# Step one's exponentials in two halves between the copies; the batch's one-hot row blocks behind its selection

## The chip, the cores and the metric

One core of a Trainium2 chip. The metric is the device time of one launch in microseconds (us); the smaller the better. The engines are TensorE (PE), VectorE (DVE), ScalarE (ACT), GpSimd (POOL) and the DMA queues that SyncE (SP) feeds. Each engine runs its own instruction stream in order; streams meet at semaphores only.

## The reference

The input is `x` (3327 nodes by 128) and `adj` (3327 by 3327, sparse in value, stored dense). First comes a graph layer with two steps (`STEPS = 2`), of which this is the core:

```python
for n in range(STEPS):
    q = Xa @ W1.T @ W2.T
    k = Xa @ W3.T
    probs = softmax(q @ k.T, axis=-1)
    # keep, in each row, the largest probabilities until their sum reaches 0.9 (ties by index)
    A = probs * mask
    A = A / A.sum(-1, keepdims=True)
    Xf = R @ Xf                      # R = (adj + I), rows normalised
    Xa = A @ Xa
    Z = Z + Xf @ U1[n].T + Xa @ U2[n].T
```

Then follow layer norms, a signed three-head graph attention over `adj`, two GRU cells and a last layer norm. The change touches only the first graph layer.

## The kernel before

Four programs run one behind the other: `layer0` (the two steps above), `normalize_and_sum`, `attention` and `gates_and_output`. Only `layer0` (L519) matters here. In it the 3327 rows, padded to `NP` = 3328, are 26 tiles of 128 rows, worked in 13 pairs (`PAIRS`), two tiles (`k` = 0, 1) to a pair. A row of logits is 3327 wide and is made in seven chunks of 512 columns (`NC` = 7, the last 256 wide).

What a pair p goes through in step one (`step == 0`):

- PE makes the logits of a tile chunk by chunk into two PSUM banks `lg` (L850). ACT copies each chunk into the tile `e` (L1152, `copy_next_logit`) and so frees its bank. A chunk's matmul waits for the copy of the chunk two before it.
- DVE takes the largest values of each segment of `e` (`tops`, MAX8 at L71), from which the row's maximum and its negative come (`negmax_ready`, L1412), and then sorts out the 48 largest (`sort_tops`, L149 to L157; `tops_ready` behind it).
- ACT turns the row into exponentials in one instruction of 3327 columns with its sum in `total` (`exps`, L1184), and the sorted values too (`exp_tops`, L1196, which waits for `tops_ready`, drains and raises `e_ready`).
- DVE searches the cut (`search`, `solve_sorted`, from L163), PE turns the flags of the search over (`turn_flags`, L902), DVE reads them (L1458) and selects (`select`, `keep` at L450), which raises `w_ready`.
- PE transposes the selected row in seven chunks into the banks `tr` (L966), ACT copies each chunk to `wT` (`copy_weights`, L1230), PE multiplies by the rows of X (L976, tile `small`), and ACT copies the outcome (`copy_row`, L1239).

The order on each engine is written out by hand. While pair p is attended, the logits of pair p + 2 are made, and pair p + 1 has its maxima, exponentials and search. In ACT's `pair`, the exponentials of tile 0 of pair p + 1 stand behind `copy_weights` chunk 4 of tile 0, and ahead of chunks 5 and 6. Those of tile 1 stand behind chunk 2 of tile 1 and ahead of the copy of logit chunk 2; `exp_tops` stands behind chunk 3. Pairs 0 to 10 and pair 12 have logit chunks between the attended ones, pair 11 has none; pair 12 has no exponentials. PE's `pair` puts logit chunks 0 and 1 ahead of attended chunk 5 of tile 0, and chunks 2 to 6 behind the attended chunks 0 to 4 of tile 1. Ahead of pair 0, the prologue makes the projections, the logits of pairs 0 and 1 and the exponentials of pair 0.

Step two (`step == 1`) has another order, in which whole exponentials stay. Rows whose nucleus its quick search can't settle are moved into one extra tile of up to 128 rows, the batch (`taken_batch`, L1526), which runs behind the 13 pairs: DVE takes fine maxima, ACT makes exponentials (L1184) and those of the candidates (L1192), DVE halves 16 times (`solve_halving`) and selects, PE attends, and last PE spreads the 128 results over the 26 tiles (`place_taken`, L953) by one-hot blocks `home`. DVE makes these 26 blocks of 128x128 in `find_homes` (L1521), between its maxima and its search, in the memory of `e[0][1]`.

Of the kernel before, what the change touches and what calls it, by code (L numbers as in the profile page):

```python
# [89 lines left out]
class Search:  # L90

    NAMES = ("total", "whole", "theta", "value", "tau", "lo", "cut", "cut_eff", "cut_kept", "above", "best", "left",
             "over", "up", "known", "reaches", "covers", "partial", "short", "strict", "backward", "cut_dropped", "scale", "levels", "shut", "mass_hi", "rowmax",
             "negmax", "open", "over_full", "spilled", "slot", "blank", "inv_kept0", "inv_kept1", "kept",
             "r_above0", "r_theta", "r_below", "r_was", "r_stays", "r_moves", "r_tau", "r_hi", "r_value", "r_bound",
             "r_above", "r_known", "r_up", "r_mass")

# [421 lines left out]
def layer0(nc, d, dims, H, ident):  # L519
# [7 lines left out]
    PROJ = 3 * NC  # L527
    FIRST_PROJ = NC + 2
    WHOLE = NC - 1
    UNITS = 2 * PAIRS  # L530
    TURN = PAIRS // 2

# [3 lines left out]
    with ExitStack() as ctx:  # L536
# [83 lines left out]
        def seq(step, p, slot):  # L620
            return (p + step * PAIRS) * 2 + slot
# [56 lines left out]
        with nc.Block() as block:  # L678
# [456 lines left out]
            def _(eng):  # L1135
# [4 lines left out]
                for step in range(2):  # L1140
# [40 lines left out]
                    def exps(p, b, k):  # L1181

                        eng.wait_ge(negmax_ready, seq(step, p, k) + 1)
                        eng.activation(e[b][k][:, 0:N], e[b][k][:, 0:N], ACT.Exp, bias=negmax[k],  # L1184
                                       accum_out=total[k])

                    def exp_tops(p):

                        eng.wait_ge(tops_ready, turn_of(step, p) + 1)
                        if at(p, PAIRS):  # L1190
                            tops = find.fine[:, :, :].rearrange("p a b -> p (a b)")
                            eng.activation(tops, tops, ACT.Exp, bias=negmax[0])  # L1192
                        for k in range(0 if at(p, PAIRS) else 2):
                            tops = (find.sorted[:, k, :] if step == 0 else
                                    find.cand[k][:, 0:SEGS[1], :].rearrange("p a b -> p (a b)"))
                            eng.activation(tops, tops, ACT.Exp, bias=negmax[k])  # L1196
                        eng.drain()
                        eng.sem_inc(e_ready, 1)
# [26 lines left out]
                    def copy_weights(p, k, c):  # L1225
                        n = seq(step, p, k) * NC + c
                        sl = cols(c)
                        eng.wait_ge(tr_ready, n + 1)
                        eng.wait_ge(wT_free, n + 1)
                        eng.activation(wT[(k * NC + c) % 2][:, 0:sl.stop - sl.start],  # L1230
                                       tr[(k * NC + c) % 2][:, 0:sl.stop - sl.start],
                                       ACT.Copy).then_inc(wT_ready, 1)
# [22 lines left out]
                    def pair(p, b, rest):  # L1255
                        ahead = rest >= 2 or at(p, PAIRS - 1)
                        for c in range(NC - 2):
                            copy_weights(p, 0, c)
                            if c == 1 and not at(p, 0):
                                copy_kq(p - 1)  # L1260
                        if rest:
                            exps(p + 1, 1 - b, 0)
                        for c in range(NC - 2, NC):
                            copy_weights(p, 0, c)
                        copy_row(p, b, 0)
                        for c in range(NC):
                            copy_weights(p, 1, c)
                            if rest and c == 2:
                                exps(p + 1, 1 - b, 1)
                            if rest and c == 3:  # L1270
                                exp_tops(p + 1)
                            if c == NC - 1:
                                copy_row(p, b, 1)
                            if ahead:
                                copy_next_logit(p, b, 0, c)
                        if ahead:
                            for c in range(NC):
                                copy_next_logit(p, b, 1, c)
                        copy_turned_attended(p)
                        copy_update(p)  # L1280
                        copy_h(p)
# [67 lines left out]
                    if step == 0:  # L1349
                        for c in range(NC):  # L1350
                            project(c, kT[0:DA, :], c)
                        project(NC, h1, 0)
                        project(NC + 1, qT[0:DA, :], 0)
                        for k in range(2):
                            copy_logits(0, 0, k)
                        for c in range(1, NC):
                            project(chunk(0, 0, 1, NC - 1) + c, h1, c)
                        for k in range(2):
                            exps(0, 0, k)
                        for c in range(1, NC):  # L1360
                            project(chunk(0, 0, 1, NC - 1) + NC - 1 + c, qT[0:DA, :], c)
                        exp_tops(0)
                        for k in range(2):
                            copy_logits(1, 1, k)
                    else:
                        for k in range(2):
                            copy_logit(0, 1, k, NC - 1)
                        copy_grid()
                        for k in range(2):
                            exps(0, 1, k)  # L1370
                        exp_tops(0)
                        for k in range(2):
                            copy_logits(1, 0, k)
# [13 lines left out]
            def _(eng):  # L1387
# [12 lines left out]
                for step in range(2):  # L1400
# [19 lines left out]
                    def search(p):  # L1420
                        eng.wait_ge(e_ready, turn_of(step, p) + 1)
                        eng.memset(gate[:, :], 0.0)
                        if step == 0:
                            find.solve_sorted(eng)
                        else:
                            find.solve_halving(eng, [find.cand[k][:, 0:SEGS[1], :].rearrange("p a b -> p (a b)")
                                                     for k in range(2)], HALVINGS)
                            find.end(eng, True, spills=True)
                        eng.sem_inc(flags_ready, 1)
# [33 lines left out]
                    def select(p, b, k):  # L1463
                        find.select(eng, k, e[b][k][:, :], kinds[k], flag, regs, step == 1,
                                    found=step == 1 and not at(p, PAIRS))
                        if step == 1:
                            eng.tensor_tensor(kept[k], kept[k], find.one("blank" if at(p, PAIRS) else "spilled", k),
                                              ALU.add)
                            eng.drain()
                        eng.reciprocal(inv_kept[b][k], kept[k]).then_inc(w_ready, 1)  # L1470
# [34 lines left out]
                        eng.wait_ge(grid_copied, 1)  # L1505
                        eng.tensor_scalar(XR[1][:, :, P], XR[1][:, :, P], row_no, None, ALU.add)

                    def find_homes():

                        eng.wait_ge(taken_copied, 1)  # L1510
                        row_of_slot = find.row_of_slot[:, :]
                        eng.tensor_copy(row_of_slot, taken_rows[:, P:P + 1])
                        eng.drain()
                        eng.tensor_scalar(row_in_tile, XR[1][:, :, P], row_no, row_of_slot, ALU.subtract, ALU.subtract)
                        eng.tensor_scalar(find.one("blank", 0), row_of_slot, 0.5, None, ALU.is_lt)
                        eng.drain()
                        eng.tensor_scalar(row_in_tile, row_in_tile, -1.0, None, ALU.mult)
                        eng.drain()
                        eng.wait_ge(tr_ready, seq(step, PAIRS - 1, 0) * NC)
                        for t in range(T):  # L1520
                            eng.tensor_scalar(home[:, t * P:(t + 1) * P], slot_no, row_in_tile[:, t:t + 1], None,  # L1521
                                              ALU.is_equal)
                        eng.drain()
                        eng.sem_inc(home_ready, 1)

                    def taken_batch():  # L1526
# [7 lines left out]
                        eng.tensor_scalar(negmax[0], rowmax[0], -1.0, None, ALU.mult).then_inc(negmax_ready, 1)  # L1534
                        eng.drain()
                        eng.sem_inc(tops_ready, 1)
                        find_homes()
                        eng.wait_ge(e_ready, turn_of(step, PAIRS) + 1)
                        eng.memset(gate[:, :], 0.0)
                        find.solve_halving(eng, [find.fine[:, :, :].rearrange("p a b -> p (a b)")], FINE_HALVINGS)  # L1540
# [8 lines left out]
                        eng.drain()  # L1549
                        eng.reg_load(kinds[0], find.flag_int[0:1, 0:1])  # L1550
                        select(PAIRS, 0, 0)
                        eng.wait_ge(addedA, 2 * PAIRS)
                        eng.wait_ge(addedR, UNITS)
                        for c in range(NC):
# [913 lines left out]
```

## Time and profile before

| what | us |
|---|---|
| median of 3 runs | 2745.24 (2742.2 to 2754.72) |
| the profiled execution | 2751.88 |
| its span | 2750.1 |
| PE busy in the span | 2367.2 (86%) |
| DVE busy | 2200.9 (80%) |
| ACT busy | 1070.2 (39%) |
| step one's pairs 0 to 11 (69.70 to 505.73) | 436.03 |
| a pair of step one, steady (216.47 to 253.36) | 36.89 |

Times in the rows are us from the span's start. A timeline row has start, length, engine, line, operation, what it writes and reads, the shape, how many such instructions are merged, and in square brackets the idle time of the engine just before and what ended it. "issue" is idle time that no recorded instruction explains. Matmuls are pipelined: in a row of several, the last one's end lies some tenths behind the start of the next group.

### The profile page before, as it was taken

To read this page: it belongs to the slowest core of one execution; us is meant where nothing else is said; L and a number is where in the kernel's file an instruction comes from. 1 tells how busy PE (TensorE), PEld (TensorE's weight loads), DVE (VectorE), ACT (ScalarE), POOL (GpSimd) and SP (SyncE) were. 2 spreads that over 40 slices of the span, in tenths; PEclk is the share of its full clock that TensorE was granted. 3 is DMA by queue.
4 is the path that set the end of the run, shared out by engine and by line. 5 is a ranking of instruction groups with operands and counts; after the bars stand their busy time and mean duration, and the time that the engine had idled before them with its cause. 6 is when DMAs were issued, how large, how long until landed. Compare 5 with 4: busy or idle time off the path is not lost. (4 is left out here: it accounts for less than half of the span.)

```text
span 2750.1 us, 53658 instructions
## 1 busy us (share of the span) xinstructions
PE 2367.2 (86%) x17795; PEld 1996.2 (73%) x17795; DVE 2200.9 (80%) x6636; ACT 1070.2 (39%) x1803; POOL 138.5 (5%) x342
## 2 busy tenths in 40 slices
PE   7999999868889887888887649987999999999985
PEld 2666666556667776767775549985999999999952
DVE  3777777588887888888889677766999999999836
ACT  4666666533323333333332130003434434434323
POOL 0000000101111111000010010000000000000000
PEclk8999999989899998999988869998999999999997
DMA  3000000022122221222221135542333343434220
GB/s 130 2 1 2 1 1 1 2 100 79 73 76 101 92 88 54 97 98 101 101 101 50 52 153 201 201 171 104 127 127 126 116 137 105 146 103 138 91 89 25
DMA packets 57330, 245.05 MB, mean 89 GB/s; under 512 B 6929, under 2 KB 18576, under 8 KB 43344
## 3 DMA queue, kind: packets, MB, share of 16 engines
q1 hardware_dynamic: 57040, 241.99, 25.2%
q8 instruction: 83, 1.36, 0.2%
q14 instruction: 207, 1.70, 0.2%
HBM read 235.15 MB, written 6.82 MB: 88 GB/s over the span
## 5 line engine op out<-in xcount | busy, mean ns | idle before, releaser
L2058 PE MATMUL a_acc<-H,pT 128*128 128x128 f32 x4056 | 548.0, 277 | 10.4 <-ACT a_rows L2090 3.8
L2058 PEld LDWEIGHTS a_acc<-H,pT 128*128 128x128 f32 x4056 | 495.5, 192 | 27.5 <-DVE pT L2192 18.7
L976 PE MATMUL small<-XR,wT 128*128 128x128 f32 x2756 | 373.3, 280 | 29.9 <-ACT wT L1230 29.3
L976 PEld LDWEIGHTS small<-XR,wT 128*128 128x128 f32 x2756 | 339.1, 195 | 45.8 <-ACT wT L1230 45.8
L850 PE MATMUL lg<-kT,qs 128*128 128x512 f32 (+1 forms) x742 | 341.0, 596 | 30.6 <-ACT e L1152 20.4
L71 DVE MAX8 cand<-e 128x8 f32<-128x64 f32 (+3 forms) x1898 | 302.8, 240 | 56.9 <-issue 34.1
L2192 DVE TENSOR_TENSOR pT<-a_tr,a_adjT 128x512 f32<-128x512 f32 (+1 forms) x546 | 316.6, 645 | 22.4 <-PE a_tr L2017 19.2
L880 PE MATMUL accR<-XR,adj 128*128 128x129 f32 x2704 | 327.9, 283 | 0.0
L880 PEld LDWEIGHTS accR<-XR,adj 128*128 128x128 f32 x2704 | 324.7, 200 | 0.0
L2017 PE MATMUL a_tr<-ident,prob 128*128 128x128 f32 x2028 | 312.4, 274 | 10.9 <-ACTq L2084 10.9
L1230 ACT ACTIVATE wT<-tr 128x512 f32<-128x512 f32 (+1 forms) x371 | 206.1, 566 | 246.7 <-PE tr L966 245.7
L2170 DVE CUSTOM_DVE_ANT_0 prob<-a_adj,EB 128x3328 f32<-128x3328 f32 x78 | 282.6, 3623 | 0.0
L850 PEld LDWEIGHTS lg<-kT,qs 128*128 128x128 f32 x742 | 119.0, 194 | 194.2 <-ACT e L1152 148.2
L966 PE MATMUL tr<-ident,e 128*128 128x128 f32 x1378 | 212.2, 281 | 48.7 <-DVE scalars L1470 42.6
L1152 ACT ACTIVATE e<-lg 128x512 f32<-128x512 f32 (+1 forms) x371 | 206.5, 566 | 114.4 <-PE lg L850 112.5
L2017 PEld LDWEIGHTS a_tr<-ident,prob 128*128 128x128 f32 x2028 | 242.1, 142 | 11.1 <-issue 11.1
L2082 ACT ACTIVATE prob<-prob,a_negmax 128x3328 f32<-128x3328 f32 x78 | 238.9, 3063 | 8.9 <-DVE a_negmax L2179 8.9
L966 PEld LDWEIGHTS tr<-ident,e 128*128 128x128 f32 x1378 | 164.8, 145 | 99.7 <-issue 55.1
L1706 PE MATMUL g_sp<-g_adj,H 128*128 128x128 f32 x1352 | 166.2, 286 | 17.2 <-ACTq L1771 17.2
L1706 PEld LDWEIGHTS g_sp<-g_adj,H 128*128 128x128 f32 x1352 | 162.0, 201 | 19.0 <-issue 18.4
L1184 ACT ACTIVATE e<-e,scalars 128x3327 f32<-128x3327 f32 x53 | 162.1, 3060 | 11.3 <-DVE scalars L1534 10.4
L219 DVE SCALAR_TENSOR_TENSOR work<-cand,mid 128x416 f32<-128x416 f32 (+1 forms) x198 | 143.3, 757 | 8.0
(344 smaller groups left out, 2485.1 us busy)
## 6 DMA issues: line engine op xcount, KB each, us to landing
adj<-in_adjT SPq DMA_DIRECT2D x52, 1664.0 KB, 7.2
g_adj<-in_adjT SPq DMA_DIRECT2D x26, 1664.0 KB, 6.8
a_adj<-in_adj SPq DMA_DIRECT2D x26, 1664.0 KB, 6.8
a_adjT<-in_adjT SPq DMA_DIRECT2D x156, 256.0 KB, 3.9
a_adjT<-in_adjT SPq DMA_DIRECT2D x26, 128.0 KB, 4.1
XT<-in_x_t SPq DMA_DIRECT2D x1, 1664.0 KB, 7.1
hT_scratch<-hT SPq DMA_DIRECT2D x1, 1664.0 KB, 12.0
nsT_scratch<-nsT SPq DMA_DIRECT2D x1, 1664.0 KB, 5.3
```

Source lines behind the costliest of these rows:

```text
L71: eng.max(cand[:, n, :], src[:, n * seg:min((n + 1) * seg, width)])
L850: eng.matmul(lg[bank(st, p, k, c)][:, 0:sl.stop - sl.start], qs[k][:, :], kT[:, sl], start=True, stop=True).then_inc(lg_ready, 1)
L880: mm = eng.matmul(accR[:, :], adj[k][:, j * P:(j + 1) * P], xf[:, j, :], start=False, stop=(j == T - 1))
L966: mm = eng.transpose(tr[(k * NC + c) % 2][:, o:o + P], e[b][k][:, j * P:(j + 1) * P], ident[:, :])
L976: mm = eng.matmul(accA[:, :], wT[(k * NC + c - 1) % 2][:, o:o + P], xa[:, j, 0:P], start=(j == 0), stop=(j == T - 1))
L1152: eng.activation(e[b][k][:, sl], lg[bank(st, p, k, c)][:, 0:sl.stop - sl.start], ACT.Copy).then_inc(lg_free, 1)
L1706: mm = eng.matmul(sp[k][:, :], H[:, j, :], adj[q][:, j * P:(j + 1) * P], start=(j == 0), stop=(j == T - 1))
L2017: mm = eng.transpose(tr[g % BANKS][:, (j % 4) * P:(j % 4 + 1) * P], prob[order[n][1]][:, j * P:(j + 1) * P], ident[:, :])
L2058: mm = eng.matmul(acc[:, :], pT[g % RING][:, (j % 4) * P:(j % 4 + 1) * P], H[:, j, :], start=(j == 0), stop=(j == T - 1))
L2082: eng.activation(prob[h][:, :], prob[h][:, :], ACT.Exp, bias=negmax[h][:, :], accum_out=den[h][:, :])
L2170: eng.tensor_tensor_reduce(prob[h][:, :], adj[k][:, :], EB[:, h, :], 1.0, -3.0e38, ALU.add, ALU.max, mx[h][:, :])
L2192: eng.tensor_tensor(pT[g % RING][:, 0:width(c)], tr[g % BANKS][:, 0:width(c)], adjT[:, c * 512:c * 512 + width(c)], ALU.mult).then_inc(pT_ ...
```

## The change

In step one the exponentials of a row are made by `exps_part` in two instructions, of 1664 and 1663 columns, with sums in `total` and in a new scalar `rest`, and the two are put between copies. For tile 0 the order on ACT becomes: weights 4, first half, weights 5, second half, weights 6. For tile 1: weights 1, first half, logit 1, weights 2, second half, `exp_tops`, logit 2, weights 3. DVE adds `rest` to `total` ahead of the search. In the prologue the two halves of a tile stand one behind the other. Step two keeps whole exponentials.

In the batch `find_homes` is cut in two: the small part (`find_blanks`) stays where it was, and the 26 one-hot blocks are made behind `select`.

```diff
@@ NAMES
-             "negmax", "open", "over_full", "spilled", "slot", "blank", "inv_kept0", "inv_kept1", "kept",
+             "negmax", "open", "over_full", "spilled", "slot", "blank", "rest", "inv_kept0", "inv_kept1", "kept",
@@ layer0
+    HALF_ROW = NP // 2
@@ scalar
+                    def exps_part(p, b, k, part):
+
+                        if part == 0:
+                            eng.wait_ge(negmax_ready, seq(step, p, k) + 1)
+                        own = slice(0, HALF_ROW) if part == 0 else slice(HALF_ROW, N)
+                        eng.activation(e[b][k][:, own], e[b][k][:, own], ACT.Exp, bias=negmax[k],
+                                       accum_out=total[k] if part == 0 else find.one("rest", k))
@@ scalar, pair
                         if rest:
-                            exps(p + 1, 1 - b, 0)
-                        for c in range(NC - 2, NC):
-                            copy_weights(p, 0, c)
+                            exps_part(p + 1, 1 - b, 0, 0)
+                        copy_weights(p, 0, NC - 2)
+                        if rest:
+                            exps_part(p + 1, 1 - b, 0, 1)
+                        copy_weights(p, 0, NC - 1)
                         copy_row(p, b, 0)
                         for c in range(NC):
                             copy_weights(p, 1, c)
+                            if rest and c in (1, 2):
+                                exps_part(p + 1, 1 - b, 1, c - 1)
                             if rest and c == 2:
-                                exps(p + 1, 1 - b, 1)
-                            if rest and c == 3:
                                 exp_tops(p + 1)
@@ scalar, prologue
                         for k in range(2):
-                            exps(0, 0, k)
+                            exps_part(0, 0, k, 0)
+                            exps_part(0, 0, k, 1)
@@ vector, search
                         if step == 0:
+                            eng.tensor_tensor(find.both("total"), find.both("total"), find.both("rest"), ALU.add)
+                            eng.drain()
                             find.solve_sorted(eng)
@@ vector, find_blanks and find_homes
-                    def find_homes():
+                    def find_blanks():
...
                         eng.tensor_scalar(row_in_tile, row_in_tile, -1.0, None, ALU.mult)
                         eng.drain()
+
+                    def find_homes():
+
                         eng.wait_ge(tr_ready, seq(step, PAIRS - 1, 0) * NC)
@@ vector, taken_batch
-                        find_homes()
+                        find_blanks()
                         eng.wait_ge(e_ready, turn_of(step, PAIRS) + 1)
...
                         select(PAIRS, 0, 0)
+                        find_homes()
                         eng.wait_ge(addedA, 2 * PAIRS)
```

## Rows read from the trace of the kernel before

**Rows 1.** Busy time by stretch: length, then each engine's busy us.
```profile
69.70:505.73 436.03, 391.21 (x2345) 278.20 (x2345) 328.40 (x1355) 274.67 (x477) 23.42 (x58) 1.00 0.01 2
```
**Rows 2.** Waits from 105 to 510 us: total us, times, longest.
```profile
DVE scalars L163 <- issue: 40.8, 11, 4.0
DVE pair_flag_int L1458 <- PE small L902: 25.9, 11, 2.5
...
PE lg L850 <- ACT e L1152: 11.4, 10, 1.1
```
**Rows 3.** Timeline of ACT in one steady pair of step one.
```profile
223.11 3.06 ACT L1184 ACTIVATE e<-e,scalars 128x3327 f32<-128x3327 f32 x1
...
226.17 1.00 ACT L1230 ACTIVATE wT<-tr 128x512 f32<-128x512 f32 x2
...
230.79 0.62 ACT L1152 ACTIVATE e<-lg 128x512 f32<-128x512 f32 x1
232.48 0.60 ACT L1230 ACTIVATE wT<-tr 128x512 f32<-128x512 f32 x1 [1.08 <-PE tr L966]
232.98 3.06 ACT L1184 ACTIVATE e<-e,scalars 128x3327 f32<-128x3327 f32 x1
...
236.03 0.58 ACT L1152 ACTIVATE e<-lg 128x512 f32<-128x512 f32 x1
...
236.98 0.56 ACT L1196 ACTIVATE sorted<-sorted,scalars 128x49 f32<-128x49 f32 x2
237.71 0.60 ACT L1152 ACTIVATE e<-lg 128x512 f32<-128x512 f32 x1 [0.16 <-issue]
```
**Rows 4.** Timeline of PE in the same pair.
```profile
225.03 0.60 PE L966 MATMUL tr<-ident,e 128*128 128x128 f32 x4
...
226.80 1.60 PE L976 MATMUL small<-XR,wT 128*128 128x128 f32 x12
...
233.18 1.02 PE L850 MATMUL lg<-kT,qs 128*128 128x512 f32 x2
...
236.66 1.13 PE L850 MATMUL lg<-kT,qs 128*128 128x512 f32 x2 [1.13 <-ACT e L1152]
```
**Rows 5.** The instructions of line L1192: durations in ns, starts.
```profile
L1192 ACT ACTIVATE cand<-cand,scalars x1: 1666/1666/1666, 1486.4 to 1486.4; 128x1664 f32<-128x1664 f32 x1
```
**Rows 6.** Timeline of PE at the prologue's exponentials.
```profile
48.29 6.20 PE L840 MATMUL lg<-XR,W2T 64*64 64x512 f32 x8 [4.95 <-ACT qT L1145]
```
**Rows 7.** Timeline in pair 0: the last of DVE's sort.
```profile
88.85 0.44 DVE L153 MAX8 sorted<-cand 128x8 f32<-128x104 f32 x2
```
**Rows 8.** Timeline in pair 0: PE at logit chunk 4.
```profile
89.22 1.12 PE L850 MATMUL lg<-kT,qs 128*128 128x512 f32 x2 [1.14 <-ACT e L1152]
```
**Rows 9.** Timeline in pair 11: DVE's sort and search.
```profile
491.39 0.44 DVE L153 MAX8 sorted<-cand 128x8 f32<-128x104 f32 x2
494.36 0.17 DVE L163 TENSOR_SCALAR scalars<-scalars 128x2 f32<-128x2 f32 x1 [2.53 <-issue]
```
**Rows 10.** Timeline in pair 11: PE's waits.
```profile
485.04 1.61 PE L976 MATMUL small<-XR,wT 128*128 128x128 f32 x12 [1.78 <-ACT wT L1230]
...
499.97 0.38 PE L902 MATMUL small<-ident,pair_flags 128*1 128x128 f32 x2 [2.02 <-DVEq L323]
...
505.73 1.50 PE L966 MATMUL tr<-ident,e 128*128 128x128 f32 x8 [3.40 <-DVE scalars L1470]
```
**Rows 11.** Timeline of the batch on ACT: exponentials of the candidates.
```profile
1486.40 1.67 ACT L1192 ACTIVATE cand<-cand,scalars 128x1664 f32<-128x1664 f32 x1
```
**Rows 12.** Timeline of the batch on DVE: the one-hot blocks and the search's gate.
```profile
1484.37 5.18 DVE L1521 TENSOR_SCALAR e<-XT 128x128 f32<-128x128 f32 x26
1489.70 0.06 DVE L1539 MEMSET gate<- 128x1 f32 x1 [0.15 <-issue]
```
**Rows 13.** Timeline of the batch on PE: attending and placing.
```profile
1559.45 1.97 PE L966 MATMUL tr<-ident,e 128*128 128x128 f32 x8 [13.86 <-DVE scalars L1470]
...
1572.94 2.02 PE L953 MATMUL lg<-zsA,e 128*128 128x128 f32 x16 [0.46 <-ACT zsA L1347]
```

## The prediction

> **What bounds the kernel now.** I read the busy time by stretch first. The pairs 0 to 11 of step one, the only loop that the split touches, take 436.03 us of the 2750.1 of the span, and PE is busy for 391.21 of them, DVE for 328.40 and ACT for 274.67 [rows 1]. So PE leads there, and only what ends PE's idle time counts. The waits of that stretch say which these are: DVE itself stands still before each search (40.8 us in 11 pairs, 3.7 each) and again until PE has turned the flags (25.9 in 11, 2.4 each) [rows 2]. DVE has slack, and a search that starts sooner brings a steady pair nothing. PE's one large wait is for the copy of a logit chunk, 11.4 us in 10 pairs, 1.14 each [rows 2]. The timelines of ACT and PE give its cause: the exponentials of tile 1 hold ACT from 232.98 to 236.03, behind them stands the copy of logit chunk 2, and PE's chunk 4 starts only at 236.66, 0.63 behind the start of that copy [rows 3, 4]. PE's own work, 1.13 less, would have been at that point by 235.53 [rows 4]. In pair 11, without logits, PE waits for weights (1.78), for the flags (2.02) and for the selection (3.40) [rows 10]: there DVE's chain leads, from the search on. In the batch DVE leads from the end of its one-hot blocks to the selection, while PE stands idle (13.86 us of it just before it attends) [rows 12, 13].
>
> **The price of a half.** A whole exponential lasts 3.06 us, and the next instruction starts 3.06 and 3.05 behind its start [rows 3], reading of the sum included. The trace has one exponential of 1664 columns from SBUF with the same bias operand: 1.67 us [rows 5]. With the same relation of length to spacing, a half costs h = 1.66, and two cost 3.32, 0.27 more than one. Ends: 1.53, half of a whole, if the fixed part vanished; 1.75, an estimate, if the reading of the sum, which the row of L1192 lacks, added a third of the fixed part of 0.27 (two halves less a whole) to it. I take 1.66.
>
> The Trainium skill, page "ScalarE: Activation LUTs", section "What ACT_TABLE_LOAD costs", gives 280 ns + 0.833 ns a column for an ACTIVATE with a pointer bias and an overlap of 93 ns between neighbours; by that a half without the reading of its sum would be spaced 1.57, and by the formula below a steady pair would change by +0.04 and not +0.31, the whole by some 3 us less. It agrees with the length of the row (1666 ns) but is silent on the sum's reading, so I keep the row.
>
> **Tile 0 of a steady pair.** The first half starts where the whole did, 223.11, and ends at 224.77. Weights 5 need PE's four transposes of 225.03, 0.60 long, so their copy starts at about 225.67 (before: 226.17, held by the exponential) [rows 3, 4]. The second half runs from 226.16 to 227.82, and only then come weights 6, 256 columns; PE can use them some 0.41 later, at 228.23 (a copy of 512 is usable 0.63 behind its start, 226.17 to 226.80, and I take 0.22 off for half the columns, an estimate). Before, both copies were out at 227.17, and PE ran the last twelve matmuls without a stop: eight of chunk 5 from 226.80 at about 0.11 each (1.60 for twelve, the last one's tail taken off), and chunk 6 from 227.69 [rows 4]. So the split frees chunk 5 by 0.23, and holds chunk 6 by 228.23 - 227.69 = 0.54. The loss is h - 1.12. All behind it on PE, tile 1's transposes included, is 0.54 later.
>
> **Tile 1.** ACT copied logit 1 at 230.79; the first half now takes that slot, at 230.79 + 0.54 = 231.33, and ends at 232.99. Logit 1 then starts at 232.99, so PE may make chunk 3 at 233.62, and wants it at 233.18 + 0.54 = 233.72 [rows 4]: just covered, by 0.10. Weights 2 follow at 233.47, the second half runs from 233.96 to 235.62. Now `exp_tops` stands ahead of logit 2, which before was behind it: from its start to the next copy are 0.73 (236.98 to 237.71) [rows 3]. Logit 2 starts at 236.35, PE's chunk 4 at 236.98, against 236.66 before. As a formula, 232.0 + 3h: three halves in a row stand in PE's way, where one whole exponential stood. Per steady pair +0.31 (ends -0.08 at h = 1.53 and +0.58 at 1.75). Ten such pairs: +3.1. Behind this point PE finds its copies ready as before. The search starts over 1 us sooner and its extra add and drain cost DVE about 0.25 (an estimate); both vanish in the 2.4 us for which DVE waits for the flags [rows 2].
>
> **Pair 0.** Here DVE's sort ends late, 88.85 + 0.44 = 89.29 [rows 7], and moves with PE. `exp_tops`, which ACT would reach at 88.2 (the steady 235.62, less the 147.44 between the two rows of PE's chunk 4 [rows 4, 8]), 1.2 us before that, now waits with logit 2 queued behind it: 89.35 + 0.73 + 0.63 = 90.71 for PE's chunk 4, against 89.22 [rows 8]. +1.5 (ends +0.3, as a steady pair, and +1.6). In the steady pairs the sort ends 3.7 - 0.6 = 3.1 before the old 236.98, at 233.9, 1.7 ahead of the new `exp_tops`: no wait.
>
> **Pair 11.** Chunk 5 no longer waits 1.78 behind the whole exponential, chunk 6 waits a little: about -0.35 [rows 10]. That alone brings nothing, since DVE leads. But the exponentials of tile 1 end sooner. The search follows the start of `exp_tops` by 0.6 (an estimate of its two instructions of 0.28, 0.56 in [rows 3], and a semaphore) and in this pair a copy of 0.49 stood between: the whole one was done by 494.36 - 0.6 - 0.49 = 493.3 [rows 9]. The first half now fills the 1.1 us for which ACT waited for transposes [rows 3]; with the 0.35 and less the 0.27 of the split, they end at about 492.1, the sort at 491.83, and the search can begin at 492.6. Less 0.25 for the add: flags, selection and pair 12 come 1.5 sooner, within the 2.02 and 3.40 for which PE waits [rows 10]. -1.5 (ends 0 and -2.0).
>
> **The prologue.** PE waits 4.95 us for the copy behind both exponentials of pair 0 [rows 6]; 2 x 0.27 = +0.54, with no cover (ends 0 and +0.8).
>
> **The batch.** The 26 blocks last 5.18 us and end at 1489.55; the search's gate runs at 1489.70. ACT's last exponential ends at 1486.40 + 1.67 = 1488.07, and with its drain and the semaphore DVE can start at 1488.3 [rows 11, 12]. -1.4. The other 3.7 us of the blocks were under ACT's exponentials anyway. Behind `select` the blocks run from the moment at which PE starts to attend, 1559.45, and end 5.5 us later, while PE asks for them at 1572.94 [rows 13]: 8 us of cover. DVE has nothing else to do there. Ends: 0 and -1.5.
>
> **The clock.** PE's first eight transposes after the wait of 13.86 lasted 1.97 [rows 13], twice what four for 0.60 make [rows 4]: it starts at the lower level. Where such a stretch ends needn't move with the work. I take 0 and keep 1.5 to both sides at the batch and again at pair 12.
>
> **Sum**, against the profiled execution's 2751.88: 3.1 + 1.5 + 0.5 - 1.5 - 1.4 = +2.2, that is 2754.1. That execution lies 6.6 above the median of the runs, 2745.24; the difference on the median gives 2747.4.
>
> **The rivals.**
> (a) The split does its work: PE's stall at chunk 4 goes, and chunk 6 isn't held. -1.14 in 11 pairs is -12.5, with pair 11, the batch and the prologue -14.9: 2730.3. For it speaks that ACT is the one that ends the wait [rows 2]. Against it: `exp_tops` was set ahead of logit 2, and a copy of 256 columns behind a half. A part of it, with h near 1.53 or an overlap that I don't see, gives -3 to -6: 2740 to 2742. Chance 0.14, of which 0.03 for the whole.
> (b) Slower: `exp_tops` waits for the sort in every pair as in pair 0. It needs a sort 1.7 us later in relation to ACT than [rows 2] say, and decides from there on. 11 x 1.5 = 16.5, with the other terms +14: 2759.3. A half of 1.75, or chunk 3 falling out of its 0.10 of cover, leads a smaller part of that way, +5 to +7: 2750 to 2752. Chance 0.18, of which 0.04 for the whole.
> (c) The batch's search isn't freed by the move, something else ending its wait at 1489.7: +1.4 on mine, 2748.9; inside the noise. Chance 0.08, and mine 0.60, with a range of its own of 2743 to 2752.
>
> The runs before spread by 12.5 us, more than any likely sum here, so the range is 2738 to 2757. A difference of under 0.5%, 13.7 us, can't be told from none. Faster by more 0.03, the same 0.92, slower 0.05.
>
> **What would show it.** In a steady pair of step one: a new wait of PE before the last matmuls of tile 0, for ACT's `wT`, about 0.6 us; the wait before logit chunk 4 still there, about 0.9; a pair of 37.2 against 36.89. In pair 0, ACT's `exp_tops` starting right at the sort's end. In pair 12, a start 1.5 sooner against pair 11. In the batch, DVE's gate 1.4 sooner, and the blocks behind the selection. I am wrong if the pair is shorter than 36.6, if the wait for weights 6 isn't there, or if the half is spaced under 1.6.

## The result and the profile after

The changed kernel took 2753.52 us (median of 6 runs, 2750.69 to 2758.76), the kernel before 2743.72 us beside it (2738.70 to 2754.72): ratio 1.0034, 95% interval 1.0018 to 1.0050. In a second measurement (12 runs against 35) it was 2752.5 against 2747.77: ratio 1.0019, interval 1.0007 to 1.0032. So it is slower by some 5 to 10 us, clear of no change, and under the 0.5% that the prediction called the same. The forecast was +2.2.

The "update" of a pair below is PE's L1005 (L1006 in the changed kernel); a pair's length is counted from one update to the next.

The profiled execution took 2758.76 us with a span of 2757.0, against 2751.88 and 2750.1. The table says where its 6.9 us lie, us from the span's start.

| point | before | after | shift |
|---|---|---|---|
| PE starts pair 0 of step one | 69.70 | 70.10 | +0.40 |
| PE at the update of pair 0 | 104.49 | 106.25 | +1.76 |
| PE starts pair 12 | 505.73 | 509.42 | +3.69 |
| DVE takes `negmax` behind the batch's maxima | 1483.14 | 1487.45 | +4.31 |
| gate of the batch's search | 1489.70 | 1492.45 | +2.75 |
| PE places the batch | 1572.94 | 1576.29 | +3.35 |
| end | 2750.1 | 2757.0 | +6.9 |

Half of the shift lies in the layer that was changed, the other half behind it, where the code is the same. That other half isn't the change's: from the placing to the end the profiles have 1177.15 us before, 1180.68 here, but 1174.58 in a second profile of the changed kernel and 1170.20 in that of the kernel with only a name added.

The first row is not a clean measure either. The prologue's split shows in PE's wait there, 5.51 us against 4.95 in [rows 6], in both profiles of the changed kernel:

```profile
49.10 6.20 PE L841 MATMUL lg<-XR,W2T 64*64 64x512 f32 x8 [5.51 <-ACT qT L1146]
```

Yet pair 0 starts 0.40 later in the first profile and, at 67.76, 1.94 earlier in the second. The stretch from the start of pair 0 to that of pair 12 repeats: 436.03 us before, 439.32 and 439.37 with the change.

The steady pair on ACT, timeline of the changed kernel. These rows answer to [rows 3].

```profile
225.40 0.60 ACT L1239 ACTIVATE wT<-tr 128x512 f32<-128x512 f32 x1 [0.73 <-PE tr L967]
225.89 1.67 ACT L1193 ACTIVATE e<-e,scalars 128x1664 f32<-128x1664 f32 x1
227.47 0.19 ACT L1193 ACTIVATION_READ_ACCUMULATOR e<-e,scalars 128x1 f32 x1
228.45 0.60 ACT L1239 ACTIVATE wT<-tr 128x512 f32<-128x512 f32 x1 [0.79 <-PE tr L967]
228.94 1.67 ACT L1193 ACTIVATE e<-e,scalars 128x1663 f32<-128x1663 f32 x1
230.51 0.19 ACT L1193 ACTIVATION_READ_ACCUMULATOR e<-e,scalars 128x1 f32 x1
230.61 0.37 ACT L1239 ACTIVATE wT<-tr 128x256 f32<-128x256 f32 x1
...
234.12 1.70 ACT L1193 ACTIVATE e<-e,scalars 128x1664 f32<-128x1664 f32 x1
...
235.78 0.61 ACT L1153 ACTIVATE e<-lg 128x512 f32<-128x512 f32 x1
236.26 0.62 ACT L1239 ACTIVATE wT<-tr 128x512 f32<-128x512 f32 x1
236.74 1.71 ACT L1193 ACTIVATE e<-e,scalars 128x1663 f32<-128x1663 f32 x1
...
238.40 0.58 ACT L1205 ACTIVATE sorted<-sorted,scalars 128x49 f32<-128x49 f32 x2
239.15 0.60 ACT L1153 ACTIVATE e<-lg 128x512 f32<-128x512 f32 x1 [0.16 <-issue]
```

A half is spaced 1.66 from what follows (234.12 to 235.78, 236.74 to 238.40); the reading of its sum starts 0.1 before its end and ends 0.1 behind the start of the next instruction. Weights 6, the copy of 256 columns, start only behind tile 0's second half; logit 2 starts behind the second half of tile 1 and behind the sorted values.

PE in the same pair, answering to [rows 4]:

```profile
229.36 1.06 PE L977 MATMUL small<-XR,wT 128*128 128x128 f32 x8
231.03 0.71 PE L977 MATMUL small<-XR,wT 128*128 128x128 f32 x4 [0.61 <-ACT wT L1239]
...
236.51 1.06 PE L851 MATMUL lg<-kT,qs 128*128 128x512 f32 x2
...
239.80 1.12 PE L851 MATMUL lg<-kT,qs 128*128 128x512 f32 x2 [0.90 <-ACT e L1153]
```

The twelve matmuls that ran without a stop are eight and four now, with 0.61 of waiting between, and the stall at chunk 4 is 0.90, where it was 1.13. The pair takes 37.24 us from one update to the next, against 36.89.

Pair 0, DVE's sort and its add, then ACT, then PE; they answer to [rows 7, 8]:

```profile
89.15 0.44 DVE L153 MAX8 sorted<-cand 128x8 f32<-128x104 f32 x2
90.32 0.16 DVE L1436 TENSOR_TENSOR scalars<-scalars 128x2 f32<-128x2 f32 x1 [0.73 <-issue]
```

```profile
89.70 0.56 ACT L1205 ACTIVATE sorted<-sorted,scalars 128x49 f32<-128x49 f32 x2 [0.99 <-DVEq L1429]
90.36 0.60 ACT L1153 ACTIVATE e<-lg 128x512 f32<-128x512 f32 x1
```

```profile
91.01 1.13 PE L851 MATMUL lg<-kT,qs 128*128 128x512 f32 x2 [1.94 <-ACT e L1153]
```

ACT stands 0.99 us until the sort has ended, with logit 2 behind it, and PE waits 1.94 us ahead of chunk 4, where it waited 1.14.

Pair 11 on PE, answering to [rows 10]: the wait for the flags went from 2.02 to 1.09, that for the selection stayed.

```profile
503.67 0.38 PE L903 MATMUL small<-ident,pair_flags 128*1 128x128 f32 x2 [1.09 <-DVEq L323]
...
509.42 1.49 PE L967 MATMUL tr<-ident,e 128*128 128x128 f32 x8 [3.40 <-DVE scalars L1484]
```

The batch on DVE, answering to [rows 12]: the search starts behind ACT's exponentials, and the blocks run behind the selection. The first line is of the kernel before and, like the second, the last instruction ahead of where the blocks stood; the search followed it by 5.59 us before and by 4.02 now.

```profile
1484.11 0.18 DVE L1517 TENSOR_SCALAR XT<-XT 128x26 f32<-128x26 f32 x1
```

```profile
1488.41 0.18 DVE L1531 TENSOR_SCALAR XT<-XT 128x26 f32<-128x26 f32 x1
1492.43 0.15 DVE L163 TENSOR_SCALAR scalars<-scalars 128x1 f32<-128x1 f32 x1 [3.84 <-issue]
```

```profile
1562.34 5.17 DVE L1538 TENSOR_SCALAR e<-XT 128x128 f32<-128x128 f32 x26
1577.57 1.48 DVE L1575 TENSOR_TENSOR H<-H,lg 128x512 f32<-128x512 f32 x2 [10.06 <-PE lg L954]
```

### The profile page after: what moved, and what is told of

Read it like the earlier page. It is cut to its first block and busy times, and to the rows that moved or that the text cites. A ratio compares the mean times of both kernels' runs of the same rounds, so it can differ in the third digit from the quotient of the medians.

```text
span 2757.0 us, 53736 instructions
## 1 busy us (share of the span) xinstructions
PE 2368.6 (86%) x17795; PEld 1999.0 (73%) x17795; DVE 2203.2 (80%) x6649; ACT 1076.5 (39%) x1855; POOL 141.5 (5%) x342
## 3 DMA queue, kind: packets, MB, share of 16 engines
q8 instruction: 83, 1.36, 0.2%
## 5 line engine op out<-in xcount | busy, mean ns | idle before, releaser
L2108 ACT ACTIVATE a_rows<-a_acc,a_inv 128x128 f32<-128x128 f32 x78 | 28.6, 367 | 226.8 <-PE a_acc L2076 226.8
```

## The experiments

My theory A: what the change costs is the order in which pieces stand ahead of the two copies that PE waits for, as summed, and what lies beyond the sum is scatter of TensorE's clock. Rivals: B, the scalar tile's 8 bytes more shift the memory layout and cost everywhere; C, the batch's move costs behind the layer; D, PE's waits move elsewhere when a piece is moved. Each kernel was run against the kernel before on the same chip. A difference in time is of medians.

**Only the name.**

```diff
-             "negmax", "open", "over_full", "spilled", "slot", "blank", "inv_kept0", "inv_kept1", "kept",
+             "negmax", "open", "over_full", "spilled", "slot", "blank", "rest", "inv_kept0", "inv_kept1", "kept",
```

> The kernel before with one more name, rest, in the list of scalars: its tile grows by 8 bytes a row, nothing else changes. Theory A (the cost is in the order of step one, about +3.7 us there and -1.5 in the batch, the rest of the measured +9.8 is scatter of the half-speed stretches of TensorE): ratio 1.000, within 3 us of before, the steady pair of step one 36.89 us. Rival B (the shifted memory layout costs some us all over the program, so that the change's +9.8 is more than its timelines show): +4 to +8 us here.

Ratio 0.9990 (0.9977 to 1.0002), 2744.0 against 2747.77; pair 36.89. The median is 3.8 below and not within 3, but the interval holds 1; rival B, which wanted +4 to +8, is out.

**Only the split** (the blocks back ahead of the search).

```diff
                         find_blanks()
+                        find_homes()
                         eng.wait_ge(e_ready, turn_of(step, PAIRS) + 1)
...
                         select(PAIRS, 0, 0)
-                        find_homes()
```

> The changed kernel with the batch's one-hot blocks put back ahead of the search. Theory A: step one's pair 37.24 us, pair 12 starts at 509.4, the batch's gate 1.4 to 1.6 us later than in the changed kernel in relation to the maxima; as a whole 1.5 us slower than the changed kernel, +3.7 or so against before in the layer, and more where the clock adds to it. Rival C (the batch's move is what costs, by what follows the layer): as fast as before plus 3.7 at most, and clearly faster than the changed kernel.

Ratio 1.0009 (0.9994 to 1.0024), 2749.77 against 2747.77. By theory A it should have been 1.5 us slower than the changed kernel; its median is 2.7 below that one's 2752.5, with intervals that overlap, so the times decide nothing here between A and C. The timelines do: pair 37.25, as in the changed kernel, and the gate behind the blocks again:

```profile
1485.74 5.18 DVE L1538 TENSOR_SCALAR e<-XT 128x128 f32<-128x128 f32 x26
1491.08 0.06 DVE L1557 MEMSET gate<- 128x1 f32 x1
```

**Only the batch.**

```diff
 # find_homes is cut in two as in the change
-                        find_homes()
+                        find_blanks()
                         eng.wait_ge(e_ready, turn_of(step, PAIRS) + 1)
...
                         select(PAIRS, 0, 0)
+                        find_homes()
```

> The kernel before with only the 26 one-hot blocks moved behind the selection. Theory A: step one as before (pair 36.89), the search of the batch 1.5 us sooner behind the maxima, the whole -1.5 us (0.9995, inside the noise). Rival C (the move of the blocks costs behind the layer, since the following parts start at another phase or on a slower TensorE): +3 to +6 us.

Ratio 0.9995 (0.9979 to 1.0011), 2747.43 against 2747.77; pair 36.89. Rival C would have had +3 to +6, of which nothing is to be seen (the interval reaches from -5.8 to +3.0 us), and its profile has 1177.06 us from the placing to the end against 1177.15 before. The -1.5 us are too small to be told by time alone. Its timeline has them: from the last small instruction to the search 4.02 us, where the kernel before had 5.59 between the same two.

```profile
1485.40 0.18 DVE L1517 TENSOR_SCALAR XT<-XT 128x26 f32<-128x26 f32 x1
1489.42 0.15 DVE L163 TENSOR_SCALAR scalars<-scalars 128x1 f32<-128x1 f32 x1 [3.85 <-issue]
```

**The changed kernel again.**

> The changed kernel as it is, measured again beside the others on the same chip. Theory A: between +2 and +7 us of before (ratio 1.001 to 1.0025), the first measurement's +9.8 having been partly scatter. Rival B or C, or another cost that the profile doesn't place: +9 to +11 again (1.0034 or more).

Ratio 1.0019 (1.0007 to 1.0032), +4.7 us in the medians. That is theory A's side, if only just by the interval's end; the first +9.8 was partly scatter.

**The sorted values behind weights 3 again.**

```diff
                             if rest and c in (1, 2):
                                 exps_part(p + 1, 1 - b, 1, c - 1)
-                            if rest and c == 2:
+                            if rest and c == 3:
                                 exp_tops(p + 1)
```

> The changed kernel with the exponentials of the sorted values back behind the copy of weights 3, so that the copy of logit 2 comes right behind the second half. Theory A (the time of a steady pair is 232.0 + 3h + what stands ahead of logit 2): PE's chunk 4 comes 0.73 sooner, the pair takes 37.24 - 0.73 = 36.5 us, 0.4 less than before; in pair 0 the wait for the sort no longer holds logit 2, another 1.2 less. Against the changed kernel -9 us, against before -5 to -6 in the layer with the batch. Rival D (what holds PE is the second half itself or the later tile 1, and the place of the sorted values is hidden): pair 37.2.

Pair 36.52 us. Ratio 0.9994 (0.9982 to 1.0007), 2746.65 against 2748.24. On PE the stall at chunk 4 is nearly gone, while the one of tile 0 stays:

```profile
224.20 0.71 PE L977 MATMUL small<-XR,wT 128*128 128x128 f32 x4 [0.62 <-ACT wT L1239]
...
232.25 1.13 PE L851 MATMUL lg<-kT,qs 128*128 128x512 f32 x2 [0.18 <-ACT e L1153]
```

One line's place was worth 0.72 us a pair, as summed (0.73); rival D fell. The time followed only in part: -1.6 us against before was measured, where -5 to -6 was expected and where pairs 0 to 11 are 5.2 us shorter in its profile. These twelve runs had a mean granted clock of 0.9338 against 0.9361 in the thirty beside them, more of a gap than their scatter explains; whether the edit brings it I can't say.

**Only tile 0 split, only step one** (the batch as before; the diff is against the changed kernel).

```diff
 # tile 0: exps_part 0, weights 5, exps_part 1, weights 6, as in the change
-                            if rest and c in (1, 2):
-                                exps_part(p + 1, 1 - b, 1, c - 1)
                             if rest and c == 2:
+                                exps(p + 1, 1 - b, 1)
+                            if rest and c == 3:
                                 exp_tops(p + 1)
```

> The kernel before with only tile 0's exponential in two halves around weights 5; tile 1 whole, the batch as before. Theory A: a wait of 0.6 us for weights 6 and 0.54 us more a pair, all of it handed through tile 1, whose stall at chunk 4 stays at 1.13: pair 37.43 us, 11 or 12 pairs, +6 us against before (1.0022). Rival D (the delay of tile 0 is taken up by the stall of 1.13 at chunk 4, since ACT leads there): pair 36.9, no difference.

Pair 37.44, ratio 1.0020 (1.0007 to 1.0032), 2752.51 against 2748.24. The delay of tile 0 is handed on in full; the stall at chunk 4 is not shortened by it:

```profile
228.47 0.71 PE L977 MATMUL small<-XR,wT 128*128 128x128 f32 x4 [0.61 <-ACT wT L1239]
...
237.44 1.13 PE L851 MATMUL lg<-kT,qs 128*128 128x512 f32 x2 [1.14 <-ACT e L1153]
```

This is the harmful half of the change.

**Only tile 1 split, with the sorted values behind weights 3 and the batch moved** (the diff is against the changed kernel).

```diff
                         if rest:
-                            exps_part(p + 1, 1 - b, 0, 0)
-                        copy_weights(p, 0, NC - 2)
-                        if rest:
-                            exps_part(p + 1, 1 - b, 0, 1)
-                        copy_weights(p, 0, NC - 1)
+                            exps(p + 1, 1 - b, 0)
+                        for c in range(NC - 2, NC):
+                            copy_weights(p, 0, c)
...
-                            if rest and c == 2:
+                            if rest and c == 3:
                                 exp_tops(p + 1)
...
-    eng.tensor_tensor(find.both("total"), find.both("total"), find.both("rest"), ALU.add)
+    eng.tensor_tensor(total[1], total[1], find.one("rest", 1), ALU.add)
```

> Tile 0's exponential whole again, tile 1's in two halves between copies, the sorted values' exponentials behind weights 3, the blocks behind the selection. Theory A: no wait for weights 6 (0.54 back), logit 2 copied at 235.07 on the steady pair's scale, PE's chunk 4 at 235.70 and not 236.66: pair 35.93 us, 0.96 less than before, and with the batch and pair 12 -11 to -13 us against before (0.9955). Rival D (PE's stall moves to another chunk, as to logit 3, which has 0.10 of cover): pair 36.4 to 36.9.

Pair 35.97, ratio 0.9964 (0.9950 to 0.9977), 2737.35 against 2748.24. It beats both kernels. Its steady pair, ACT then PE:

```profile
224.98 1.69 ACT L1193 ACTIVATE e<-e,scalars 128x1664 f32<-128x1664 f32 x1
...
227.12 0.62 ACT L1239 ACTIVATE wT<-tr 128x512 f32<-128x512 f32 x1
227.59 1.71 ACT L1193 ACTIVATE e<-e,scalars 128x1663 f32<-128x1663 f32 x1
...
229.26 0.62 ACT L1153 ACTIVATE e<-lg 128x512 f32<-128x512 f32 x1
```

```profile
220.99 1.60 PE L977 MATMUL small<-XR,wT 128*128 128x128 f32 x12
...
229.93 1.12 PE L851 MATMUL lg<-kT,qs 128*128 128x512 f32 x2 [0.18 <-ACT e L1153]
```

They say why a split that costs 0.27 pays here. Ahead of weights 2 ACT stood idle for 1.08 us [rows 3]; the first half now fills that time, weights 2 follow without a wait, and so the second half ends, and logit 2 comes, some 0.95 sooner than behind the whole exponential. Run again:

> The kernel with tile 1 split alone, measured again beside the one with tile 0 earlier. Theory A: pair 35.97 us, ratio 0.995 to 0.997, -9 to -13 us against before, as the first time. Rival E (its first ratio was luck of the half-speed stretches): 0.998 or more.

Ratio 0.9952 (0.9935 to 0.9970), 2737.18 against 2748.22; pair 35.98. The gain repeats, and rival E is out.

**Nothing split, tile 1's exponential behind logit 2**, the sorted values behind logit 3, the batch moved (the diff is against the kernel before and leaves out the batch).

```diff
-                            if rest and c == 2:
-                                exps(p + 1, 1 - b, 1)
-                            if rest and c == 3:
-                                exp_tops(p + 1)
...
                             if ahead:
                                 copy_next_logit(p, b, 0, c)
+                            if rest and c == 2:
+                                exps(p + 1, 1 - b, 1)
+                            if rest and c == 3:
+                                exp_tops(p + 1)
```

> The kernel before, nothing split: tile 1's whole exponential stands behind the copy of logit 2 and the sorted values' behind that of logit 3; the blocks behind the selection. Theory A (order is what counts, not length): PE's chunk 4 no longer waits (1.13 back), chunk 3's weights come 0.2 late: pair 35.95 to 36.0 us, -10 to -12 us against before. Rival D (one piece of 3.05 us holds PE somewhere anyway): the stall reappears in front of weights 3 or logit 5, pair 36.5 to 36.9, -1.5 us in all.

Pair 36.08, ratio 0.9984 (0.9972 to 0.9996), 2742.94 against 2748.24. PE has one wait in its place, for weights 3:

```profile
233.74 1.16 PE L976 MATMUL small<-XR,wT 128*128 128x128 f32 x8 [0.33 <-ACT wT L1230]
```

So nearly all of the pair's gain of the kernel with tile 1 split (0.92) is had without a split (0.81), by order alone. The time gained 5.3 us where 10 to 12 were expected, half of what the kernel with tile 1 split gained in the same measurement. Its mean granted clock was lower than that of the runs beside it, 0.9343 against 0.9361. In its profile pair 12 took 40.89 us, against 37.9 to 38.6 in the other kernels; the granted clock stood at its lower level, 1.2 GHz, from 495 to 500, and the mean of the pair was 0.83, against 0.89 in the kernel with tile 1 split (37.97 us):

```profile
492.57:533.50 40.93, 36.58 (x194) 26.73 (x193) 14.98 (x62) 16.65 (x33) 7.16 (x7) 0.83 0.01 1
495.00:500.00 5.00, 3.39 (x15) 3.16 (x16) 4.90 (x4) 1.20 (x2) 4.74 (x3) 0.50 0.01 3
```

These are busy times by stretch, the third column from the right being the granted clock. PE's first transposes of the pair:

```profile
496.61 1.97 PE L966 MATMUL tr<-ident,e 128*128 128x128 f32 x8 [2.99 <-DVE scalars L1470]
```

Whether each run of that kernel has this I can't say; the profiled run, 2734.74 us, is one of its fastest.

**Tile 0's exponential behind weights 3** (on top of the kernel with tile 1 split).

```diff
                             if c == 1 and not at(p, 0):
                                 copy_kq(p - 1)
-                        if rest:
-                            exps(p + 1, 1 - b, 0)
+                            if rest and c == 3:
+                                exps(p + 1, 1 - b, 0)
```

> The kernel with tile 1 split alone, tile 0's whole exponential one chunk earlier, behind weights 3. Theory A: PE's stall of 0.23 ahead of chunk 5's matmuls goes, weights 4 come just in time for theirs (a start 0.63 ahead of PE's want): pair 35.97 - 0.2 = 35.75 us, 2 to 3 us less than the kernel with tile 1 split alone, 0.9955 of before. Rival D (weights 4, now behind the exponential, come late by as much as chunk 5 gains): pair 35.95 or more, no gain.

Pair 35.76, ratio 0.9945 (0.9924 to 0.9966), 2735.35 against 2748.22, the lowest median of all. The pair's 0.21 is shown by the timelines; the 1.8 us below the kernel with tile 1 split are not clear of none (6 runs against 7, spread by 11 and 9 us). Weights 4 follow the exponential and are just in time:

```profile
215.73 3.06 ACT L1185 ACTIVATE e<-e,scalars 128x3327 f32<-128x3327 f32 x1
218.69 0.19 ACT L1185 ACTIVATION_READ_ACCUMULATOR e<-e,scalars 128x1 f32 x1
218.78 0.59 ACT L1239 ACTIVATE wT<-tr 128x512 f32<-128x512 f32 x1
219.62 0.60 ACT L1239 ACTIVATE wT<-tr 128x512 f32<-128x512 f32 x1 [0.25 <-PE tr L967]
```

## Why the prediction held, and where its sum was small

| step | predicted | measured |
|---|---|---|
| spacing of a half | 1.66 | 1.66 |
| wait for weights 6 | about 0.6 | 0.61 |
| wait ahead of chunk 4 | about 0.9 | 0.90 |
| steady pair | +0.31, 37.2 | +0.35, 37.24 |
| ten pairs | +3.1 | +3.5 |
| pair 0 | +1.5 | +1.36 |
| pair 11 | -1.5 | -1.53 |
| prologue, PE's wait | +0.54 | +0.56 |
| pairs 0 to 11 together | +3.1 | +3.29, second profile +3.34 |
| start of pair 12 | +3.6 | +3.69, second profile +1.40 |
| batch's search | -1.4 | -1.56 |

**The half's price.** The row of 1664 columns was the right one to take, and the reading of the sum hides behind it: 0.19 long, spaced 1.66 with it. The Trainium skill (page "ScalarE: Activation LUTs", section "What ACT_TABLE_LOAD costs") has 280 ns + 0.833 ns a column and an overlap of 93 ns, and says nothing of the reading of a sum. The estimate from it, +0.04 a pair, isn't what the trace has, +0.35: the length of a half, 1.67, agrees, but two instructions spaced 1.57 by it are spaced 1.66 here, with the reading behind each.

**Tile 0 and tile 1.** Both steps hold as worked. The kernel with tile 0 split alone shows the first (+0.55 a pair), the one with the sorted values moved the third term (0.72 of 0.73), the one with tile 1 split both away (-0.92; expected -0.96). Chunk 3, which I called covered by 0.10, was: PE shows no wait there.

**Pair 0 and pair 11.** ACT's wait for the sort was 0.99 us and cost what was summed. In pair 11 the search began sooner, and the add with its drain cost 0.24 (90.32 to 90.56 in pair 0) as estimated.

**The batch.** The move gains 1.56 and its cover at the end holds: the blocks end at 1567.5, the placing asks at 1576.3.

**The sum.** For pairs 0 to 11 it is right to some 0.2 us in both profiles, and for the prologue's wait to 0.02. That the start of pair 12 came out right to 0.05 (3.69 against 3.1 + 0.54) owes something to chance: in the second profile that point lies 2.3 us earlier, by a shorter start of the program (the granted clock from 20 to 30 us was 1.00 there, and 0.83 in the kernel before and in the first profile). Up to the batch's search the layer stands at +2.75; the 0.6 that step two adds is scatter, since the kernel with only a name added has the same 0.6 there. What the sum hadn't is behind the layer: 3.5 us in the profiled execution, on code that is the same. The records of the granted clock have 143.0 us at the lower level behind the layer, against 136.4. The prediction put such stretches at nothing and kept 1.5 us to each side at two places; they scatter over the whole program and by more (1169.69 to 1181.10 us from the placing to the end, over the profiles).

As a median +4.7 and +9.8 were measured where +2.2 was forecast. The direction is the sum's. The first median, 2753.52, lies inside the range of 2738 to 2757, which was drawn as wide as the scatter, and 1.5 above the range of 2743 to 2752 that the prediction gave to its own mechanism; what bears the mechanism out is the timelines, not that number. The rival (a), faster by the stall of 1.14, is refuted as the change stands, and so is the whole of (b): only pair 0 shows ACT's wait for the sort. The prediction was right too about why the gain wasn't had: with tile 0 left whole and the sorted values left in place, the stall does go.

What stays open is some 2 us. Within a kernel, over 181 runs, a run's time falls by 1.8 us for 0.001 more of mean granted clock (correlation -0.81, each run taken against its own kernel's mean). The table has the means against before, brought to one clock with that slope, beside what the timelines say (the prologue's wait, pairs 0 to 11, the batch's search). A number of the middle column is uncertain by about 1 us either way, as a standard error.

| kernel | at one clock | by its timeline |
|---|---|---|
| name | -1.2 | 0 |
| batch alone | -1.3 | -1.6 |
| split alone | +5.8 | +3.9 |
| the change, second measurement | +4.5 | +2.3 |
| tile 0 split | +6.2 | +6.2 |
| sorted values behind weights 3 | -5.7 | -6.2 |
| nothing split | -9.0 | -10.6 |
| tile 1 split, and again | -11.8, -13.6 | -12.1 |
| tile 0 earlier | -13.6 | -14.4 |

The kernels fall in the order of their timelines, and the batch's share fits. The change and the split alone both stand 2 us above theirs, about twice the standard error, and no run here says why. The correction takes the clock as something that befalls a kernel. Two kernels (sorted values behind weights 3, nothing split) had it lower than the runs beside them by 0.002, so an edit may itself move it; that isn't shown either way, and without the correction these two gained 1.6 and 5.3 us only.

## What to carry to other kernels

Cutting a long instruction in two pays where the first piece fills time in which its engine stood idle, so that the second ends sooner than the whole did. In tile 1 it filled 1.08 us, and the cut gained 0.92 a pair. In tile 0 there was no such time: the second piece only held up a copy that had been ready, and the cut cost 0.55. So count, for each awaited copy, what stands ahead of it before and after, idle time included. A small reordering with no split at all gave nearly all of the gain in the pair's length, though in the median only half of the gain in time. And a neighbour moved along with it (the sorted values' exponentials, 0.73 us, and their own wait) can cost more than the cut.

## What the runs showed of the hardware

- An exponential of 1664 columns is spaced 1.66 us from the next instruction, one of 3327 columns 3.06: the fixed part is 0.27 (two halves less a whole). The reading of the accumulated sum has a row of its own of 0.19, and overlaps its neighbours by 0.1 on each side.
- The scatter of a kernel's time, 9 to 22 us between its 12 runs here, goes with TensorE's clock: in the twelve profiles the stretches at the lower level (1.2 GHz) sum to 334.5 to 372.1 us. They differ as much for code that is the same: 371.7 and 348.3 in the two profiles of the changed kernel, 355.1 with only a name added and 368.5 before. A difference of 5 us was only just clear of none with 12 runs against 30.
- The same eight transposes at pair 12's start took 1.49 us in the changed kernel, and 1.97 in the one with nothing split, behind a shorter wait (2.99 against 3.40): where the lower level falls didn't follow the length of the wait in these two.
